# Four graph layers on one core: the nodes' loops taken out of the edge list on chip

## The chip, the cores and the metric
The kernel runs on one core of a Trainium2 chip. The metric is device time in microseconds: before the change the median of three runs is 5938.38 us (5931.77 to 5943.11). The engines are PE (TensorE), DVE (VectorE), ACT (ScalarE), POOL (GpSimd) and SP (SyncE), each with its own instruction stream; they meet at semaphores.

## The reference, cut to what matters
There are 6250 nodes with 256 features. The edge list has 106250 entries, sorted by destination: 100000 random ones (50000 drawn and their reverses) and one loop for each node. The sort is stable and the loops were appended last, so a node's loop is the last entry of that node. Four layers follow one another; each has the form

```
h = max(layernorm(x), 0);  x = x + layer(h, src, dst)
L0 (hyperbolic): agg = segment_sum(logmap(h[src], h[dst]) * edge_weight, dst), then row-wise Moebius steps
L1 (attention):  g = direction * magnitude of h @ W.T + b;  score = g[src] @ a_s + g[dst] @ a_t
                 agg = segment_sum(g[src] * softmax_over_dst(score), dst);  out = ball(g + agg)
L2:              g = h @ W; e = exp(-leaky_relu(g[r] @ a1 + g[c] @ a2, 0.2)); out = elu(sum(e * g[c]) / sum(e))
L3 (mean):       out = h @ w_self.T + b_self + (segment_sum(h[src], dst) / degree) @ w_neigh.T
```
In L0 a loop's term is zero (logmap of a point at itself). In L1, L2 and L3 a loop's term is the node's own row with its own factor.

## The kernel before, in words
Nodes lie in 49 blocks of 128. X (the running x), H (the rows that are gathered or added) and A (the sums) each hold all blocks in SBUF, 256 features wide, H and A with three more columns (AUX to AUX3) for scores, squares and sums of factors.

**Set-up** (DVE from L1001, PE from L494, SP from L331). The list is 831 tiles of 128 edges (ET). A tile that crosses from one block into the next gets one step for each, which makes 831 + 48 = 879 steps, padded to S = 880. DVE builds a matrix `pick` of tiles against steps and PE multiplies the split integers with it (L513) to get the tables src_tab, dst_tab, w_tab and block_tab, one column a step. In the meantime DVE takes the statistics of x (L1064), and ACT normalizes (norm_first, L843) and squares (square_first, L848). SP stores the rows of the first layer to the DRAM table in seven parts (store_part, L361), after it has written the lists of steps out. A is cleared by POOL (L483) when those have landed.

**A pass** is one layer's walk over the steps. In each step POOL gathers the 128 source rows by an indirect DMA out of the table (gathers_layer0, L464, into a ring of 48 slots; gathers, L472, ring of 40), a weighted one-hot matrix of the destinations is made (DVE compares, ACT weighs), PE multiplies it with the gathered rows (sum_step0, L570; sum_step, L577), and DVE adds the product from PSUM to the step's block of A (add_sum, L1133). Where the step starts a new block, the factor same_tab is 0 and the old contents of A are dropped. POOL waits on the semaphore `used`, which PE raises for each ring slot that it has read.

- Pass 1 (L0) works in groups of 16 steps. DVE takes the dot products of gathered rows with own rows two groups ahead (own_dot, L1229), the distances one group ahead (edge_distances, L1250), so the first sum needs two groups of gathers.
- Pass 2 (L1) works in groups of 20 steps. Each group's softmax maxima are found along the rows by scans and linked across rows; a running sum is faded where a block goes on into the next group (fade_first). best_scores (L1534) adds a table not_own that masks a node's own score. In the last 49 steps finished blocks are divided by their totals (totals, L1585) and added to H (combine, L1590), one a step; ACT squares them (square_sum).
- Pass 3 (L2) is alike with its own exponents (leaky_exponents, L1653), and finished blocks go through elu steps on ACT and DVE.
- Pass 4 (L3) needs no weights.

After each pass norm_pipe (L1512) updates X, normalizes, and PE multiplies with the next weights; SP stores the new table. POOL starts the next pass when the seven parts have landed. The order of the work inside a pass is written out by hand, step by step, for each engine.

Of the kernel before, what the change touches and what calls it, by code (L numbers as in the profile page):

```python
# [30 lines left out]
S_REAL = ET + NB - 1  # L31
ITERS = -(-S_REAL // RING)
S = ITERS * RING
assert S - S_REAL <= 1
SH = S // 2
UN = 7
assert ITERS % 2 == 1
# [14 lines left out]
LATE = 17  # L52
# [4 lines left out]
SUM_LAG = HOTS + 2  # L57
# [3 lines left out]
NG0 = S // GR0  # L61
# [6 lines left out]
assert S % GR0 == 0 and SLOTS0 * W <= NB * D and 4 * OWN <= SLOTS  # L68
FAR = 1 << 20
# [7 lines left out]
def gnn_program(nc, x, src, dst, edge_weight, w0, bias0, w1, b1, mag_w, mag_b, attn_w, w2, a2,  # L77
                w_neigh, w_self, b_self, out):
    with ExitStack() as ctx:
# [50 lines left out]
        ident_b = sb("ident_b", [P, P], BF16)  # L130
# [5 lines left out]
        own_dram = nc.dram_tensor("own_dram", [P, S], F32, kind="Internal").ap()  # L136
# [56 lines left out]
        not_own = w_tab[:, :]  # L193
# [19 lines left out]
        fade_1 = e_flat[:, 10 * GR + 9:10 * GR + 10]  # L213
        is_first = e_flat[:, 10 * GR + 10:10 * GR + 10 + NG]
        assert 10 * GR + 10 + NG <= 18 * RING
        pick = a_flat[:, 0:EC * S // 2].bitcast(BF16).rearrange("p (c s) -> p c s", c=EC)
        iota_s = a_flat[:, EC * S:EC * S + S]
        t0_ = EC * S + S
        turned_dst = a_flat[:, t0_:t0_ + EC * P].rearrange("p (c e) -> p c e", c=EC)
        t0_ += EC * P  # L220
        rows_out = a_flat[:, t0_:t0_ + EC * P // 2].bitcast(BF16).rearrange("p (c e) -> p c e", c=EC)
        t0_ += EC * P // 2
        cuts_out = a_flat[:, t0_:t0_ + EC * (P + 2) // 2].bitcast(BF16).rearrange("p (c e) -> p c e", c=EC)
        t0_ += EC * (P + 2) // 2
        own_out = a_flat[:, t0_:t0_ + S]
        t0_ += S
        links_out = a_flat[0:1, t0_:t0_ + 3 * CW // 2].bitcast(BF16).rearrange("p (n s) -> p n s", n=3)
        t0_ += 3 * CW // 2
        assert t0_ <= NB * W and CW % 2 == 0
        o = 0  # L230
        rows_i, parts_of = {}, {}
        for name in ("dst", "src"):
            rows_i[name] = h_flat[:, o:o + EC * P].bitcast(I32).rearrange("p (c e) -> p c e", c=EC)
            o += EC * P
# [84 lines left out]
        def batch_in(eng, q, i, j, ahead=0):  # L319

            eng.wait_ge(sem(f"batch_in{j}"), i * (16 * BATCH) + 16 * BATCH * (q * TURNS + 1 + ahead))
# [170 lines left out]
        def _(pe):  # L492
# [13 lines left out]
            for n, name, made in ((0, "dst", 1), (3, "tile", 1), (1, "src", 2), (2, "w", 3)):  # L506
                pe.wait_ge(sem("parts_made"), made)
                terms = [(t[:, c, :], c) for t in parts_of[name] for c in range(EC)]
                if name == "tile":
                    terms += [(tile_low, c) for c in range(EC)]  # L510
# [1366 lines left out]
```

## Time and profile before
| what | value |
| --- | --- |
| median of 3 runs | 5938.38 us |
| lowest, highest run | 5931.77, 5943.11 us |
| profiled execution, first to last instruction (span) | 5110.8 us |
| own time of the profiled execution beyond the span | not given; the median lies 827.6 us above the span |
| busy PE, DVE, ACT, POOL | 3290.4, 3431.6, 1841.1, 3349.8 us |
| mean granted TensorE clock | 0.810 of full speed |
| gathers (indirect DMAs of POOL) | 3520, 467.01 MB |

A busy share is an average over four passes and the stretches between them, in which different engines work. Which engine ends a stretch has to be read from the waits and from the timeline. DMA issues and semaphore waits are not counted as busy, except POOL's indirect DMAs, whose descriptors POOL makes itself.

### The profile page before, as it was taken

The page shows a single profiled execution, that of the slowest core. Times are in us where ns is not written, and L with a number is a line of the kernel's source. Part 1 is how long each engine was busy: PE and PEld are TensorE (multiplying, and loading weights), DVE is VectorE, ACT ScalarE, POOL GpSimd, SP SyncE. Part 2 cuts the span into 40 slices and gives each one's busy share as a digit, 9 for nine tenths or more (in the row PEclk, how much of TensorE's full clock was granted, in tenths as well). Part 3 has the DMA queues.
Part 4 walks back from the last instruction along what each step waited for, and adds up shares of the span by engine and source line. Part 5 has one row for each costly group of instructions (what it writes and reads, how often), then busy time and mean ns, then how long its engine had stood idle before and what let it go on. Part 6 is the DMA issues. An engine that isn't in the chain of part 4 may idle for free. (4 is left out here: it accounts for less than half of the span.)

```text
span 5110.8 us, 58785 instructions
## 1 busy us (share of the span) xinstructions
PE 3290.4 (64%) x11755; PEld 2256.4 (44%) x11755; DVE 3431.6 (67%) x10603; ACT 1841.1 (36%) x4370; POOL 3349.8 (66%) x3529
## 2 busy tenths in 40 slices
PE   2788888887444655566655666666666666666666
PEld 1556666655332333333334444444444444444444
DVE  7799999999974666666676555555558455555556
ACT  2455555555782333333344333333337100000000
POOL 1777777774007777777752777777772577777776
PEclk7899999998776777777777888888877877778787
DMA  4444444444024333333445554555554444443434
GB/s 137 136 133 132 134 133 133 133 133 120 11 91 124 107 107 107 107 107 107 107 117 153 132 132 132 132 132 134 133 133 141 138 114 114 114 114 107 113 107 142
DMA packets 302511, 617.15 MB, mean 121 GB/s; under 512 B 66649, under 2 KB 175189, under 8 KB 302166
## 3 DMA queue, kind: packets, MB, share of 16 engines
q0 software_dynamic: 168960, 467.01, 34.5%
q1 hardware_dynamic: 107862, 117.55, 7.5%
q10 hardware_dynamic: 25344, 28.85, 2.0%
q8 instruction: 113, 1.85, 0.1%
q14 instruction: 232, 1.90, 0.1%
HBM read 560.58 MB, written 52.57 MB: 120 GB/s over the span
## 5 line engine op out<-in xcount | busy, mean ns | idle before, releaser
L478 POOL DMA_INDIRECT X<-table,src_tab x2640 | 2500.7, 947 | 1360.5 <-issue 752.1
L585 PE MATMUL psum<-X,onehot 128*128 128x259 f32 x5280 | 1847.6, 494 | 905.8 <-ACT onehot L722 333.6
L1142 DVE SCALAR_TENSOR_TENSOR A<-A,same_tab,psum 128x259 f32 x3476 | 1671.8, 481 | 756.9 <-PE psum L585 531.8
L585 PEld LDWEIGHTS psum<-X,onehot 128*128 128x128 f32 x5280 | 1169.2, 241 | 1376.9 <-ACT onehot L722 582.4
L468 POOL DMA_INDIRECT X<-table,src_tab x880 | 836.9, 951 | 280.7 <-issue 251.6
L722 ACT ACTIVATE onehot<-G,zero_col,ecols 128x128 f32<-128x128 bf16 x1760 | 730.0, 481 | 688.9 <-PE psum L585 451.3
L594 PE MATMUL psum<-H,G 128*128 x1760 | 603.1, 429 | 249.6 <-DVE G L1238 196.3
L574 PE MATMUL psum<-X,onehot 128*128 128x259 f32 x1760 | 567.6, 407 | 4.2 <-ACT onehot L722 2.2
L594 PEld LDWEIGHTS psum<-H,G 128*128 128x128 f32 x1760 | 323.7, 205 | 429.0 <-issue 392.1
L722 ACT ACTIVATE onehot<-onehot,zero_col,coef 128x128 f32<-128x128 bf16 x880 | 365.9, 481 | 128.7 <-DVE coef L1281 103.1
L1238 DVE SCALAR_TENSOR_TENSOR G<-psum,X 128x257 f32<-128x257 f32 x880 | 367.1, 418 | 61.8 <-DMA X<-table,src_tab 38.0
L722 ACT ACTIVATE ecols<-ecols,zero_col 128x20 f32<-128x20 f32 (+2 forms) x187 | 52.4, 302 | 987.5 <-DVE ecols L1663 486.9
L574 PEld LDWEIGHTS psum<-X,onehot 128*128 128x128 f32 x1760 | 357.5, 204 | 71.3 <-issue 10.7
L992 ACT COPY onehot<-psum 128x256 f32<-128x256 f32 x49 | 18.2, 372 | 1020.0 <-PE psum L560 1020.0
L1129 DVE TENSOR_TENSOR G<-psum,dst_tab 128x1280 bf16<-128x1280 f32 x176 | 261.3, 1485 | 34.6 <-ACT onehot L722 34.5
L1245 DVE TENSOR_SCALAR onehot<-iota_b,dst_tab 128x128 bf16<-128x128 bf16 x880 | 230.0, 261 | 0.0
L623 PE MATMUL psum<-ident,ecols 128*20 128x128 f32 x44 | 17.0, 387 | 308.5 <-DVE ecols L1539 308.5
L1657 DVE TENSOR_REDUCE ecols<-psum 128x20 f32<-128x60 f32 x44 | 9.7, 221 | 292.0 <-DMA X<-table,src_tab 292.0
L722 ACT ACT_TABLE_LOAD x137 | 175.8, 1283 | 77.5 <-DVE mv L1072 61.3
L1538 DVE TENSOR_TENSOR ecols<-X,w_tab 128x20 f32<-128x20 f32 x44 | 8.2, 186 | 264.3 <-DMA X<-table,src_tab 264.3
L1129 DVE TENSOR_TENSOR onehot<-psum,dst_tab 128x640 f32<-128x640 f32 x176 | 144.1, 819 | 43.6 <-issue 33.4
L616 PE MATMUL psum<-wide_rows,onehot 128*128 x880 | 131.6, 237 | 58.0 <-issue 38.4
(347 smaller groups left out, 2826.0 us busy)
## 6 DMA issues: line engine op xcount, KB each, us to landing
X<-table,src_tab POOLq DMA_INDIRECT x3520, 2.8
plain<-rows_dram SPq DMA_DIRECT2D x110, 256.0 KB
plain<-rows_dram ACTq DMA_DIRECT2D x176, 160.0 KB, 3.4
table<-H SPq DMA_DIRECT2D x21, 906.5 KB, 8.5
x_dram<-X SPq DMA_DIRECT2D x21, 896.0 KB, 4.1
X<-x_dram SPq DMA_DIRECT2D x14, 896.0 KB, 5.1
X<-in_x SPq DMA_DIRECT2D x2, 6144.0 KB
table<-A SPq DMA_DIRECT2D x7, 906.5 KB, 7.2
```

The costliest lines, as they stand in the source:

```text
L468: pool.indirect_dma_start(ring0[:, s % SLOTS0, :], None, table, bass.IndirectOffsetOnAxis(src_tab[:, s:s + 1], 0)).then_inc(sem(f"batch0_{ ...
L478: pool.indirect_dma_start(ring[:, s % SLOTS, :], None, table, bass.IndirectOffsetOnAxis(src_tab[:, s:s + 1], 0)).then_inc(sem(f"batch_in{s ...
L574: pe.matmul(psum[:, s % ACC_BANKS, 0:W], hots0[:, s % HOTS0, :], ring0[:, s % SLOTS0, :], start=True, stop=True).then_inc(sem("used"), 1)
L585: pe.matmul(psum[:, k % ACC_BANKS, 0:W], hots[:, k % HOTS, :], ring[:, k, :], start=True, stop=True).then_inc(sem("used"), 1)
L594: pe.matmul(psum[:, 4 + s % 4, 0:D + 1], oht[:, s // B0 % 2, s % B0, :], blk(H, at, 0, D + 1), start=True, stop=True).then_inc(sem("own_ro ...
L616: ins = pe.matmul(psum[:, 4 + h, c * OWN:c * OWN + P], hot_t[:, first % 2, k, :], u_parts[:, bass.ds(vs[k] * OWN, P)], start=True, stop=True)
L722: return act.activation(out_, in_, f, **kw)
L992: act.copy(late_v, late_turned).then_inc(sem("late_kept"), 1)
L1129: return tt(out_, numbers.rearrange("p (o n) -> p o n", o=1).to_broadcast([P, n, P]), dst_tab[:, bass.ds(first, n)].rearrange("p (s o) -> ...
L1142: stt(total, total, same, psum[:, t % ACC_BANKS, 0:W], ALU.mult, ALU.add).then_inc(sem("sum_added"), 1)
L1238: stt(junk0[:, q, k % 2, at:at + D + 1], psum[:, 4 + s % 4, 0:D + 1], 1.0, ring0[:, s % SLOTS0, 0:D + 1], ALU.mult, ALU.mult, accum_out=en ...
L1245: ts(equal0[:, s % GR0, :], iota_b[:, :], dst_tab[:, s:s + 1], None, ALU.is_equal).then_inc(sem("equal_0"), 1)
```

## The change
The loops are taken out of the list on chip. DVE packs destination-in-block and source of each edge into one word, clears each node's last entry, and moves every word left by the number of loops before it in its block (its destination's number in the block), in seven conditional shifts by 1, 2, 4, ... 64. Every block then loses exactly 128 entries, and what crosses a row's left edge is added to the row before: each of the 830 rows of 128 has edges of one block alone. POOL moves the weights in the same seven rounds with DVE's masks. The rows are turned by PE into the tables. S is 840; pass 1 walks S0 = 832 steps, the others 830.

The own terms come from SBUF: in pass 2 the sums carry their peak in AUX3 and are merged with the node's own row in three groups of blocks (MERGES: 0-14, 14-28, 28-49), in pass 3 ACT writes own rows times own factor into A before the sums, in pass 4 A holds the own rows already; in passes 3 and 4 add_sum always adds (factor 1.0). The set-up is reordered: x is loaded by ACT's queue in seven parts at once, its statistics come part by part after the words are moved, A is cleared first, the four weights are loaded and turned last, and the lists of steps are written out after the table's parts.

```diff
-S_REAL = ET + NB - 1
-S = ITERS * RING
-LATE = 17
+S_REAL = E // P
+LT = -(-(E - N) // P)
+S = 840
+LATE = 16
+MERGES = ((0, 14), (14, 28), (28, NB))
+S0 = 832
+LOW = [P + 1 - (1 << i) for i in range(7)]
 # SP
-            sp.wait_ge(sem("edges_padded"), 6)
-            (dst, src, w: 9 loads; prev_i: 7 loads; then weights, vectors, x in 2 loads)
+            rows_in("dst", dst, dst_rows_i[:, :, 0:P], "edges_in")
+            for c in range(EC): (first number of the next row, 7 loads)
+            rows_in("src", src, src_rows_i, "edges_in")
+            sp.wait_ge(sem("sums_zero"), 1)
+            rows_in("w", edge_weight, w_rows[:, :, P:2 * P], "w_in")
...
 # POOL
+            pool.memset(A[:, :, :], 0.0).then_inc(sem("sums_zero"), 1)
+            def move_weights():
+                pool.wait_ge(sem("w_in"), 16 * 3)
+                pool.wait_ge(sem("words_made"), 1)
+                now = w_rows[:, :, P:2 * P]
+                pool.tensor_tensor(now, now, keep_rows, ALU.mult).then_inc(sem("w_kept"), 1)
+                for i, low in enumerate(LOW):
+                    shift = 1 << i
+                    pool.wait_ge(sem("movers"), i + 1)
...
+                    now, to = w_rows[:, :, low:], w_rows[:, :, low - shift:2 * P - shift]
+                    pool.tensor_copy(moved_w[i], movers[i])
+                    pool.tensor_tensor(moved_w[i], now, moved_w[i], ALU.mult)
+                    pool.tensor_tensor(now, now, moved_w[i], ALU.subtract)
+                    pool.tensor_tensor(to, to, moved_w[i], ALU.add)
...
+            def scale_own(lo, hi):
+                pool.wait_ge(sem("shares"), len(MERGES))
+                for b in range(lo, hi):
+                    pool.tensor_scalar(H[:, b, 0:D], H[:, b, 0:D], col("be")[:, b:b + 1], None, ALU.mult).then_inc(sem("own_scaled_late"), 1)
-            pool.wait_ge(sem("steps_out"), 16 * (2 * EC + 2))
-            pool.memset(A[:, :, :], 0.0).then_inc(sem("sums_zero"), 1)
+            pool.wait_ge(sem("src_kept"), 1)
             pool.wait_ge(sem("table_stored"), 16 * OUTER)
             gathers_layer0()
 # ACT
+            for c in FIRST_ORDER:
+                act.dma_start(X[:, a:z, :], x[a * P:z * P, :]...).then_inc(sem(f"x_part{c}"), 16)
...
+            def merges(s):
+                for m, (lo, hi) in enumerate(MERGES[:-1]):
+                    at = s - (LT + hi)
+                    if at == 4: merge_parts(m)
+                    if 0 <= at - 8 < hi - lo: scale_own(m, lo + at - 8)
+                    if 0 <= at - 14 < hi - lo: square_sum(lo + at - 14)
...
+                    for b in range(NB):
+                        func(A[:, b, :], H[:, b, :], ACT.Identity, scale=col("be")[:, b:b + 1]).then_inc(sem("own_rows"), 1)
 # DVE
-            pick, number_parts, bn_stats of all x, tables from PE's products
+            chain(stt(first, delta_i, float(1 << SRC_BITS), src_rows_i, ALU.mult, ALU.add))
+            chain(stt(first, first, float(REAL << SRC_BITS), keep_rows, ALU.add, ALU.mult))
+            for i, low in enumerate(LOW):
...
+                chain(ts(movers[i], now, SRC_BITS + i, 1, ALU.logical_shift_right, ALU.bitwise_and))
+                chain(tt(taken, now, movers[i], ALU.mult))
+                chain(tt(now, now, taken, ALU.subtract))
+                chain(tt(to, to, taken, ALU.add))
+            first_stats(0)
+            for n in range(1, OUTER):
+                first_stats(n)
+                first_rstd(n - 1)
...
             def add_sum(q, i, t, at, same=None):
+                if q > 0:
+                    same = 1.0
...
             def best_scores(i, h):
-                chain(tt(tg, at[:, :, AUX3], not_own[...], ALU.add))
-                tt(cand, tg, at[:, :, AUX2], ALU.max)
+                dve.tensor_copy(cand, ring[:, h % 2 * GR:h % 2 * GR + GR, AUX2])
...
+            def merge_gaps(m):    (nine operations on lo:hi columns)
+            def merge_shares(m):  (seven operations on lo:hi columns)
+            def merges(s):
+                    if at == 0: merge_gaps(m)
+                    if at == 6: merge_shares(m)
+                    if 0 <= at - 10 < hi - lo: combine(lo + at - 10)
...
-            totals(OUTER - 1)
-            for b in range(S - ET - UN, NB):
-                combine(b)
+            merge_gaps(len(MERGES) - 1)
+            for m, (lo, hi) in enumerate(MERGES[:-1]):
+                for b in range(max(lo, lo + S_REAL - LT - hi - 10), hi):
+                    combine(b)
+            merge_shares(len(MERGES) - 1)
+            for b in range(*MERGES[-1]):
+                combine(b)
```

## Rows read from the trace of the kernel before

**Rows 1.** Groups by line, all of the span: busy us, mean ns | idle us before, releasers.

```profile
L478 POOL DMA_INDIRECT X<-table,src_tab x2640 | 2500.7, 947 | 1360.5 <-issue 752.1 <-DMA table<-H 438.0 <-DMA table<-A 119.2
...
L468 POOL DMA_INDIRECT X<-table,src_tab x880 | 836.9, 951 | 280.7 <-issue 251.6 <-PE psum L574 16.1 <-DMA table<-H 13.0
```

**Rows 2.** Timeline of POOL: start us, us, what [idle before <-releaser].

```profile
126.10 1.11 POOL L468 DMA_INDIRECT X<-table,src_tab  x1 [12.99 <-DMA table<-H]
...
1229.79 0.94 POOL L468 DMA_INDIRECT X<-table,src_tab  x1 [0.30 <-issue]
...
1542.30 0.94 POOL L478 DMA_INDIRECT X<-table,src_tab  x1 [311.57 <-DMA table<-H]
...
2641.25 0.94 POOL L478 DMA_INDIRECT X<-table,src_tab  x1 [0.30 <-issue]
...
2768.63 0.94 POOL L478 DMA_INDIRECT X<-table,src_tab  x1 [126.44 <-DMA table<-H]
...
5091.00 0.95 POOL L478 DMA_INDIRECT X<-table,src_tab  x1 [0.30 <-issue]
```

**Rows 3.** Stretches, passes 1 and 2: busy PE, PEld, DVE, ACT, POOL, clock, DMA.

```profile
171.00:1230.00 1059.00, 875.65 (x3379) 651.79 (x3379) 975.23 (x4380) 616.76 (x1212) 801.91 (x845) 0.93 0.49 132
...
1575.00:2642.00 1067.00, 644.40 (x2035) 390.57 (x2035) 676.66 (x1703) 384.77 (x960) 807.20 (x854) 0.77 0.40 108
```

**Rows 4.** Waits of all engines: us in total, times, longest.

```profile
DVE ecols L1538 <- DMA X<-table,src_tab: 264.3, 44, 19.3
...
DVE G L1238 <- DMA X<-table,src_tab: 38.0, 41, 5.0
```

**Rows 5.** One line, the sums of pass 1: duration ns, first and last start.

```profile
L574 PE MATMUL psum<-X,onehot x1760: 379/382/772, 171.6 to 1259.0; 128*128 128x259 f32 x196
```

**Rows 6.** Timeline of the set-up, DVE, ACT, PE and SP.

```profile
15.12 0.23 DVE L1020 CAST ident_b<-ident 128x128 bf16<-128x128 f32 x1 [10.22 <-DMA H<-in_dst]
...
34.24 0.62 DVE L1039 TENSOR_SCALAR H<-H 128x896 int32<-128x896 int32 x1
...
37.33 1.09 DVE L1058 TENSOR_TENSOR H<-H 128x896 f32<-128x896 f32 x1
...
43.95 16.11 DVE L1064 BATCH_NORM_STATS2 G<-X 128x6 f32<-128x256 f32 x49 [3.74 <-DMA X<-in_x]
...
63.72 3.55 ACT L722 ACTIVATE H<-X,cols 128x256 f32<-128x256 f32 x7 [0.77 <-DVE cols L1075]
...
74.24 1.75 PE L519 MATMUL psum<-ident,dst_tab 128*128 128x128 f32 x7 [14.28 <-DVEq L1093]
...
92.93 6.99 ACT L722 ACTIVATE H<-X,cols 128x256 f32<-128x256 f32 x14 [5.03 <-DVEq L1124]
...
100.54 14.37 SPq L362 DMA_DIRECT2D table<-H  x7
```

**Rows 7.** Timeline around POOL's memset and behind it.

```profile
102.44 10.67 POOL L483 MEMSET A<- 128x12691 f32 x1 [100.04 <-DMA links_dram<-A]
...
102.73 0.42 DVE L1183 SCALAR_TENSOR_TENSOR G<-H 128x256 f32<-128x256 f32 x1
...
103.46 9.69 DVE L1187 COPY cols<-H 128x49 f32<-128x49 f32 x1 [0.30 <-ACT onehot L722]
...
123.19 0.19 DVE L1216 TENSOR_SCALAR cols<-cols 128x49 f32<-128x49 f32 x1
...
125.85 0.21 DVE L1219 COPY H<-cols 128x49 f32<-128x49 f32 x1 [2.47 <-DMA table<-H]
```

**Rows 8.** Timeline, end of pass 2 and start of pass 3.

```profile
2679.00 0.47 DVE L1142 SCALAR_TENSOR_TENSOR A<-A,same_tab,psum 128x259 f32 x1
...
2680.22 2.86 DVE L1591 SCALAR_TENSOR_TENSOR A<-A,cols,H 128x256 f32<-128x256 f32 x7
...
2683.70 0.49 ACT L722 ACTIVATE wide_rows<-A,zero_col 128x256 f32<-128x256 f32 x1
...
2795.51 0.22 DVE L1657 TENSOR_REDUCE ecols<-psum 128x20 f32<-128x60 f32 x1 [15.21 <-DMA X<-table,src_tab]
```

More of the change, by code:

```diff
@@ L268, in blocks_at, with base, batch_turns @@
                 skip_runtime_bounds_check_because="set-up clamps the steps' blocks to NB - 1")[1]
+        def base(q):
+            return S0 + q * S if q >= 0 else 0
+        def batch_turns(j):
+            return sum(i * SLOTS + j * BATCH < S_REAL for i in range(TURNS))
         block = ctx.enter_context(nc.Block())
@@ new lines, in _ @@
+            sp.wait_ge(sem("edges_padded"), 2)
+            rows_in("dst", dst, dst_rows_i[:, :, 0:P], "edges_in")
+            with nc.allow_non_contiguous_dma(reason="one number of each row"):
+                for c in range(EC):
+                    n = min(P, ET - 1 - c * P)
+                    sp.dma_start(dst_rows_i[0:n, c, P:P + 1], dst[(c * P + 1) * P:(c * P + n) * P + 1:P].rearrange("(p c) -> p c", c=1)
+                                 ).then_inc(sem("edges_in"), 16)
+            rows_in("src", src, src_rows_i, "edges_in")
@@ L488, in _ @@
                 gathers(q)
+                if q == 0:
+                    scale_own(*MERGES[-1])
         @block.tensor
@@ L985, in _ @@
             weighted(1)
-            for b in range(S - ET - ELU_LAG, NB + 1):
+            for b in range(S_REAL - LT - ELU_LAG, NB + 1):
                 elu_parts(b)
@@ new lines, in _, with first_stats @@
+            dve.sem_inc(sem("words_moved"), 1)
+            dve.memset(H[:, :, AUX], -0.5)
+            chain(dve.memset(H[:, :, AUX3], 0.0))
+            dve.sem_inc(sem("aux_kept"), 1)
+            def first_stats(n):
+                c = FIRST_ORDER[n]
+                dve.wait_ge(sem(f"x_part{c}"), 32 if c == OUTER - 1 else 16)
+                for b in part(c):
+                    ins = dve.bn_stats(out=stats0[:, b, 0:6], in_=X[:, b, :])
+                chain(ins)
+                now = part_of(stats0, c)
+                m0, m1, v0, v1 = now[:, :, 1], now[:, :, 4], now[:, :, 2], now[:, :, 5]
+                two, odd, off = part_of(col("t0"), c), part_of(col("t1"), c), part_of(col("t2"), c)
+                tt(off, m0, m1, ALU.subtract)
+                tt(odd, v0, v1, ALU.add)
+                chain(tt(two, m0, m1, ALU.add))
+                chain(stt(off, off, 0.25, off, ALU.mult, ALU.mult))
+                stt(mv[:, c * UN:c * UN + UN, 1], odd, 1.0 / D, off, ALU.mult, ALU.add).then_inc(sem("var_ready"), 1)
@@ L1838, in _ @@
             chain(dve.memset(A[:, :, AUX:W], 1.0))
-            for b in range(S - ET - 10, NB):
+            for b in range(S_REAL - LT - 10, NB):
                 weighed(b)
```

595 lines of the change are left out of this document (337 added, 258 removed).

## The prediction
> **What bounds the kernel now.** I read first the costliest groups of the page, and there the gathers: one GpSimd (POOL) indirect DMA per step, 2640 in three passes and 880 in the first, each busy 0.95 us, with nearly all the idle time before them put down to "issue" [rows 1]. Then the timeline of POOL alone, for the first and the last gather of each pass: the first pass runs from 126.10 to 1229.79, so 879 periods of 1.2556 us; the second from 1542.30 to 2641.25, 879 periods of 1.2502 us [rows 2]. The last gather of the kernel starts at 5091.00, 19.8 us before the end of the span. So in all passes POOL issues without a stop, at 0.95 us + 0.30 us of its own issue; a pass costs 880 of these periods. Third, the table of stretches: in the first pass DVE is busy 975 of 1059 us (92%), in the second 677 of 1067 (63%), PE and ACT less [rows 3]. Fourth, the waits: DVE waits 264 us for gathered rows in the second pass and only 38 us in the first [rows 4]. POOL sets the time in every pass; in the first DVE is close behind it: its own pace is about 1.2556 - 38/880 = 1.21 us a step. Between passes POOL is idle 311.6, 126.4 and 119.2 us, and 126 us before the first.
>
> **The steps that go.** The first pass keeps 832 of 880 gathers, the others 830. On the path: 48 x 1.2556 = 60.3 us and 150 x 1.2502 = 187.5 us, together 247.8 us. Nothing else can take their place in passes 2 to 4: in pass 2 the busiest other engine is idle for a third of the time [rows 3], and the page's slices show no more in passes 3 and 4. PE, ACT and DVE lose the same steps; that is worth nothing there.
>
> **Set-up, the part that can give some back.** Before, the table of the first pass is what POOL waits for: the edges are in at 15.1; picking the tiles (DVE 20 to 32) and PE's matmuls run until the input x has landed at 43.9 and its 49 statistics are done at 60.1; ACT normalizes from 63.7 on and is held at the last two parts and a half by the DVE's tables until 92.9; the seven stores of 0.9 MB go out from 100.54 and have landed at 126: 3.6 us each [rows 2, 6].
>
> After, x is asked for at once by ACT's queue, beside the edge lists (13 small DMAs of SP). Before, 15 edge DMAs were in 11 us after the first issue [rows 6]; with x beside them I take 20 us for the words' start (low 16, high 27). Then DVE has seven rounds over 7 chunks of 128, 129, 131, 135, 143, 159, 191 columns: in all 7112 columns, 7.94 times the 896 of the rows shown. A round is one operation with one input (0.63 us for 896) and three with two inputs (1.09 us) [rows 6], 3.9 us; 7.94 x 3.9 + 28 waits of 0.05 = 32 us. POOL does the same rounds on the weights: one copy and three two-input operations. No row has such an operation on POOL. Its nearest row is the memset of 12691 columns in 10.67 us, 0.84 ns each [rows 7]. One stream a column is the low end; two reads and a write one after the other, 2.5 ns, the high end. I take 2.1 for the two-input ones (between two and three streams) and 0.84 for the copy: 7112 x (3 x 2.1 + 0.84) = 51 us; ends: 24 and 60.
>
> **Do the two take turns?** In the trace a DVE copy of 49 columns, which took 0.21 us at 125.85, lasted 9.69 us at 103.46: it started under POOL's memset and ended with it [rows 7]. A two-input DVE operation that started 0.3 us into that memset took its normal 0.42 us [rows 7]. So the one-input operations of the rounds wait for POOL's whole instruction; of the two-input ones the row only says that they don't mind a POOL instruction that merely writes. POOL's rounds read as well. I take it that all take turns, one for one, since both queues chain their steps and each leaves the other a gap: 32 + 51 = 83 us, and the words are moved at about 20 + 83 = 103, the weights at 104. If only the one-input operations wait, it is 20 + 32 + 7 copies of POOL or so = 60, and the weights at 75.
> The Trainium skill, "SBUF — State Buffer", section "SBUF: two separate sides", says that DVE's second pair of ports is GpSimd's only one, an exclusive lock held for a whole instruction, and that a DVE operation with two SBUF inputs contends with a GpSimd operation that reads SBUF. By that rule all the rounds take turns, 83 us and not 40; the trace shows its first half (the 9.69 us), no row here shows the second. "GPSIMD Engine Reference", section "Elementwise — side-by-side cycle accounting", gives 4497 ns for a two-input f32 operation of 2048 columns; by that figure the POOL rounds would be an estimated 53 us.
>
> **First gather.** After the words are moved (103): one part of x's statistics 2.3 (a seventh of 16.11), its small operations 0.9, the second part's of both before the first reciprocal 3.2, reciprocal and start 1 (the root with its table load lies beside it): ACT starts at 111. It has 49 normalizations of 0.51 (7 in 3.55 us) [rows 6] and 21 squares of 0.49 [rows 8], with seven roots 37 us: 148. The last part's store adds 3.6 + 2: the first gather at 154, against 126.1: **+28**.
>
> **First sum.** DVE's own list behind it: 7 parts x 3.7 us of statistics (129), tables 5, the 28 row squares, which end with ACT's order at about 141, the block row 4, so the tables stand at 145. From there before, at 74.2, to the cuts kept at 92.9 it was 18.7 us [rows 6]; it gets two more matmuls and four row operations (+5), then the weights' turn and table 6, the four weight copies 3 (moved from the front), and the chain of small operations that took 10.0 us from 113.2 to 123.4 [rows 7]. That is 145 + 43 = 188, 34 us after the first gather. Before, DVE stood ready at the first gather and the first sum came 45 us later (171.6) [rows 5], held by 32 gathers. Now the 32 gathers are there, and DVE, PE and ACT need by their own pace about 36 us: the first sum at 224. POOL's ring of 48 is full at 154 + 60 = 214, and it goes on when four sums are done, at 228: **+14**. From there on 784 periods of 1.2556: the last gather at about 1212, against 1229.8. DVE's 1.21 us a step lets it keep up. So of 60.3 us the first pass gives 18 and the set-up eats 42 (bounds from the unknowns: 0 with no turns at all, 60 with 2.5 ns and edges at 27).
>
> **Between second and third pass.** Before, the last sum ends at 2679.5, 7 sums are combined until 2683.1, ACT's last square is done at 2684.2 [rows 8], 43 us after the last gather. After, the last merge group is 21 blocks and all of it comes behind the last sum. The last sum itself stays near 38 us after the last gather: the last group has 10 steps, not 20, but ACT has per step a weighing, a scaling and a square, 1.46 us instead of 0.97. Then nine small DVE operations (1.7), two exponentials (0.7), seven more (1.4), and 21 blocks at POOL's pace: 256 columns, 0.3 us at the memset's rate, 0.65 at 2.1 ns, and DVE's 0.48 us combine (two inputs) either beside it or in turn with it: 10 to 24 us; I take 15, plus the last square 1. Sum 38 + 3.8 + 15 + 1 = 58 against 43: **+14** (5 to 24).
>
> **Start of the third pass.** 49 own rows on ACT, 49 x 0.51 = 25 us, from about 2774 on in the old count: done at 2799. The exponents wait for 20 gathers anyway until 2795.5 [rows 8]. 3 us late, and POOL's ring of 40 has 50 us: **0**. If that cover were gone it would be 25.
>
> **At no cost.** The extra operations of a group in pass 2 (a copy, two one-column operations) lie in DVE's 37% idle time, with 6 us of waiting for gathers in each of 44 groups [rows 3, 4]. End of passes 3 and 4: the same 48 or 49 blocks follow the same last gathers; ACT bounds the tail of pass 3 before and after (0, at most -5 or +5). Pass 4: one more mean behind its last sum, +0.5.
>
> **Sum.** -247.8 + 42 + 14 + 0.5 = -191 us on the profiled execution, whose span is 5110.8; the page gives no other time of it. The median of the runs is 827.6 us more than this span. What lies there isn't in the trace; I take it as unchanged: 5938.4 - 191 = **5747 us**, span 4920. If it goes with the number of steps, it loses up to 198/3520 of 828 = 47 us.
>
> **Rivals.** (1) No turns, or few: the two-input operations of DVE and POOL run side by side. For: the 0.42 us row. Against: POOL's rounds read, the memset doesn't. The words are at 60, all behind is 43 us earlier, total 5704. (2) DVE is the bound of the whole first pass: it starts 34 us behind POOL and 92% busy; if its pace is 1.2556 and not 1.21, the last sum comes at 224 + 1045 = 1269 instead of 1241: 5775. For: 92%. Against: the 38 us it waits. (3) The steps are free for POOL but the time around the span shrinks with the program: 5700. Nothing in the profile speaks for or against. (4) Slower: POOL's moving of the weights. It is one chain in set-up, and every sum waits for its last step. Break-even is where it takes 191 us more than my 51: 242 us for 28448 columns, 8.5 ns a column, ten times the memset's rate. For: none of these forms is in the trace, POOL is a slow engine for them if they convert and overlap in place. Against: 0.84 ns in the only row. It gives over 5940, by 12 ns 6040. (5) It doesn't do what it says, POOL's period grows as gathers of empty slots (6250 of them, all to row 0) hit one row: needs 1.25 to 1.31 us. Against: the time from a gather's issue to its data is not on POOL.
>
> **Chances.** Forecast 0.60 (own range 5725 to 5770); rival 1 0.20; rival 2 0.10; rival 3 0.06; rivals 4 and 5 together 0.04. Range: down to rival 1 and a little of 3, up past rival 2 and POOL at 2.5 ns with late edges: 5685 to 5795. A measurement of this kernel tells 0.2% (12 us) from no change. Faster by more: 0.95; within: 0.02; slower: 0.03.
>
> **What would show it.** Right: 832 and 3 x 830 gathers at 1.25 us without waits but for one of some 14 us at the 49th; DVE's two-input operations in the rounds at 2 to 3 us instead of 1.09 to 1.6; first gather near 154, first sum near 224; the gap between passes 2 and 3 near 140 us. Wrong: DVE's rounds at normal length (rival 1); waits of POOL for PE all through pass 1 (rival 2); a POOL operation of over 8 us in the rounds (rival 4); the span 191 us shorter but the time by another amount (rival 3).

## The result, and the profile after

| runs | before, us | after, us | ratio |
|---|---|---|---|
| first timing | 5935.08 (5924.34 to 5943.11) | 5719.18 (5710.40 to 5728.73) | 0.9635 [0.9619, 0.9652] |
| later (experiments 1 and 2) | 5108.73 (5106.85 to 5112.72) | 4942.97 (4942.24 to 4945.48) | 0.9675 [0.9662, 0.9689] |

After is 216 us faster in the first timing, where 191 were predicted. The second line is from the experiments, and it changes how the first is read. Some executions are held up again and again for some 3 us at a time, here called stops; others, of the same kernel, never are. The trace of before that stood ahead of the prediction (span 5110.8 us) is of an execution without stops, while its runs took 5935 us; from the experiments it follows that the 827.6 us that the prediction put "around the span" are such stops, though no trace of before holds them. The first trace of after has them: its span is 5726.9 of its 5728.73 us. This is its timeline of all engines in one stop of the second pass (start, length, engine, line, operation, tiles, in brackets the idle time before and what ended it):

```profile
2501.58 0.30 PEld L639 LDWEIGHTS psum<-X,onehot 128*128 128x128 f32 x2 [1.44 <-issue]
2502.09 0.95 POOL L519 DMA_INDIRECT X<-table,src_tab  x1 [0.30 <-issue]
2505.05 1.26 ACT L780 ACTIVATE onehot<-G,zero_col,ecols 128x128 f32<-128x128 bf16 x3 [3.39 <-remote]
2505.22 1.11 DVE L1280 SCALAR_TENSOR_TENSOR A<-A,same_tab,psum 128x259 f32 x2 [2.36 <-remote]
2505.33 0.94 POOL L519 DMA_INDIRECT X<-table,src_tab  x1 [2.29 <-remote]
2505.82 0.50 PEld L639 LDWEIGHTS psum<-X,onehot 128*128 128x128 f32 x2 [3.95 <-ACT onehot L780]
```

ACT, DVE, POOL and PE all start again within 0.8 us, after 2.3 to 4 us. The releaser "remote" says only that no record of the releaser is there: the traces with stops hold 24600 to 25900 records of semaphore updates, those without 77600 to 81600. Of the intervals between POOL's gathers within the passes, 300 are over 2 us; the median stays 1.254. In 298 of the 300 the next gather is one ahead of which POOL waits on the semaphore `used` (in pass 1 every fourth from the 49th on, later every fifth); the other two are among the first ten gathers. So POOL is held at its waits and not at any place, and the other engines are not always still then: during 138 of the 300 all of them start nothing for 1.5 us or more, during 117 one of them starts something at least every 1 us.

The second trace of after (span 4943.4 us) has no stops and is the one to lay beside the rows of before. Its page and its costliest groups on POOL:

```profile
span 4943.4 us, 56247 instructions
PE 3104.0 (63%) x11120; PEld 2145.1 (43%) x11120; DVE 3249.0 (66%) x10287; ACT 1807.0 (37%) x4285; POOL 3270.2 (66%) x3382
...
L519 POOL DMA_INDIRECT X<-table,src_tab x2490 | 2372.3, 953 | 1273.5 <-issue 711.3 <-DMA table<-H 396.0 <-DMA table<-A 119.6
L509 POOL DMA_INDIRECT X<-table,src_tab x832 | 794.5, 955 | 307.9 <-issue 235.8 <-DMA table<-H 50.8 <-PE psum L626 21.3
```

These answer to [rows 1]: 2490 + 832 gathers instead of 2640 + 880, each still 0.95 us. POOL's timeline in that trace, the first and last gather of each pass and the 49th of the first, answers to [rows 2]:

```profile
155.59 1.21 POOL L509 DMA_INDIRECT X<-table,src_tab  x1 [50.79 <-DMA table<-H]
222.18 0.94 POOL L509 DMA_INDIRECT X<-table,src_tab  x1 [3.63 <-PE psum L626]
1206.22 0.95 POOL L509 DMA_INDIRECT X<-table,src_tab  x1 [0.30 <-issue]
1518.52 0.94 POOL L519 DMA_INDIRECT X<-table,src_tab  x1 [311.36 <-DMA table<-H]
2554.91 0.95 POOL L519 DMA_INDIRECT X<-table,src_tab  x1 [0.30 <-issue]
2713.15 1.01 POOL L519 DMA_INDIRECT X<-table,src_tab  x1 [84.66 <-DMA table<-H]
3760.11 0.95 POOL L519 DMA_INDIRECT X<-table,src_tab  x1 [0.31 <-issue]
3880.62 0.95 POOL L519 DMA_INDIRECT X<-table,src_tab  x1 [119.56 <-DMA table<-A]
4924.65 0.95 POOL L519 DMA_INDIRECT X<-table,src_tab  x1 [0.31 <-issue]
```

From these starts and those of before comes the ledger (us, from first to last gather for a pass, from last to first for a gap):

| stretch | before | after | change | predicted |
|---|---|---|---|---|
| to the first gather | 126.1 | 155.6 | +29.5 | +28 |
| pass 1 | 1103.7 | 1050.6 | -53.1 | -60.3 + 14 = -46 |
| gap 1 to 2 | 312.5 | 312.3 | 0 | 0 |
| pass 2 | 1099.0 | 1036.4 | -62.6 | -62.5 |
| gap 2 to 3 | 127.4 | 158.2 | +30.9 | +14 |
| pass 3 | 1102.2 | 1047.0 | -55.2 | -62.5 |
| gap 3 to 4 | 120.6 | 120.5 | 0 | 0 |
| pass 4 | 1099.6 | 1044.0 | -55.6 | -62.5 |
| behind the last gather | 19.8 | 18.8 | -1.0 | +0.5 |
| sum (span) | 5110.8 | 4943.4 | -167 | -191 |

The gap between passes 2 and 3 is off by 17 us, passes 3 and 4 by 7 us each, and pass 1 by 7 the other way. The other 50 us of the 216 are stops: they cost before 5935.1 - 5108.7 = 826 us and after 5719.2 - 4943.0 = 776.

### The profile page after: what moved, and what is told of

Same layout as the page of the kernel before. It is cut to its first block and busy times, and to the rows that moved or that the text cites. A ratio compares the mean times of both kernels' runs of the same rounds, so it can differ in the third digit from the quotient of the medians.

```text
span 5726.9 us, 56247 instructions
## 1 busy us (share of the span) xinstructions
PE 3325.1 (58%) x11120; PEld 2190.7 (38%) x11120; DVE 3240.2 (57%) x10287; ACT 1822.4 (32%) x4285; POOL 3263.8 (57%) x3382
## 3 DMA queue, kind: packets, MB, share of 16 engines
q0 software_dynamic: 159456, 440.74, 29.5%
## 5 line engine op out<-in xcount | busy, mean ns | idle before, releaser
L519 POOL DMA_INDIRECT X<-table,src_tab x2490 | 2367.9, 951 | 1799.0 <-issue 695.8
L639 PE MATMUL psum<-X,onehot 128*128 128x259 f32 x4980 | 1917.1, 525 | 1270.9 <-DVE A L1280 621.5
L639 PEld LDWEIGHTS psum<-X,onehot 128*128 128x128 f32 x4980 | 1130.2, 253 | 1848.1 <-issue 1055.4
L1280 DVE SCALAR_TENSOR_TENSOR A<-A,psum 128x259 f32 x1660 | 701.6, 423 | 1325.8 <-remote 723.0
L1280 DVE SCALAR_TENSOR_TENSOR A<-A,same_tab,psum 128x259 f32 x1620 | 776.8, 480 | 579.4 <-remote 259.0
L509 POOL DMA_INDIRECT X<-table,src_tab x832 | 792.6, 953 | 535.2 <-issue 232.0
L780 ACT ACTIVATE onehot<-G,zero_col,ecols 128x128 f32<-128x128 bf16 x1660 | 699.3, 482 | 994.6 <-remote 324.9
L626 PE MATMUL psum<-X,onehot 128*128 128x259 f32 x1664 | 557.8, 421 | 4.4 <-DVE A L1280 3.1
L780 ACT ACTIVATE onehot<-onehot,zero_col,coef 128x128 f32<-128x128 bf16 x832 | 350.4, 482 | 275.3 <-DVE coef L1411 93.2
L626 PEld LDWEIGHTS psum<-X,onehot 128*128 128x128 f32 x1664 | 353.8, 214 | 74.2 <-issue 9.5
L1368 DVE SCALAR_TENSOR_TENSOR G<-psum,X 128x257 f32<-128x257 f32 x832 | 346.9, 417 | 17.4 <-remote 8.4
L814 ACT CAST G<-G 128x1024 f32<-128x1024 bf16 x104 | 107.8, 1037 | 180.0 <-PE psum L648 85.5
L670 PEld LDWEIGHTS psum<-wide_rows,onehot 128*128 128x128 bf16 x840 | 83.2, 104 | 155.1 <-issue 132.4
```

The source lines that it names most:

```text
L509: pool.indirect_dma_start(ring0[:, s % SLOTS0, :], None, table, bass.IndirectOffsetOnAxis(src_tab[:, s:s + 1], 0)).then_inc(sem(f"batch0_{ ...
L519: pool.indirect_dma_start(ring[:, s % SLOTS, :], None, table, bass.IndirectOffsetOnAxis(src_tab[:, s:s + 1], 0)).then_inc(sem(f"batch_in{s ...
L626: pe.matmul(psum[:, s % ACC_BANKS, 0:W], hots0[:, s % HOTS0, :], ring0[:, s % SLOTS0, :], start=True, stop=True).then_inc(sem("used"), 1)
L639: pe.matmul(psum[:, k % ACC_BANKS, 0:W], hots[:, k % HOTS, :], ring[:, k, :], start=True, stop=True).then_inc(sem("used"), 1)
L670: ins = pe.matmul(psum[:, 4 + h, c * OWN:c * OWN + P], hot_t[:, first % 2, k, :], u_parts[:, bass.ds(vs[k] * OWN, P)], start=True, stop=True)
L780: return act.activation(out_, in_, f, **kw)
```

## The experiments

After's time without stops is 4942.97 us; "gap" is the one between passes 2 and 3, 158.2 us in after.

**1. Before again, unchanged.** 

> The kernel before, unchanged, once more, for a second trace. In the trace shown of before the span is 5110.8 us though the kernel's runs take about 5935, and none of its intervals between gathers in a pass is over 1.6 us; in the trace of after the span is 5726.9 of 5728.7 us, and all engines stop together about 300 times for some 3 us (711.9 us beyond 1.25 us a gather, and more in the gaps). Theory A: every timed execution holds such stops, and the first trace of before was of an execution without them: the span is now 5925 to 5945 us, a pass of 880 gathers lasts 1240 to 1360 us instead of 1100 to 1104, the stops hold 700 to 830 us, and an average step costs 1.43 to 1.50 us where the prediction took 1.25. Theory B: the 827.6 us lie around the span in before's executions as the prediction took it: the span is again about 5111 us, with no interval over 1.6 us, and a step costs 1.25 us.

Span 5118.2 us, no interval over 1.6 us, a step 1.253 to 1.260 us: B's numbers. But before's nine timed runs beside it had a median of 5108.73, so nothing lies around the span and B's reason is wrong; A is wrong in that not every execution has stops. At three later times, each on another chip, before's median was 5107.7, 5869.5 and 5922.0. Each chip was met once, so whether the chip makes the stops, or something else that changed between the times, is not shown.

**2. After again, unchanged.** 

> The kernel after, unchanged, timed beside the next two kernels, and for a second trace. 5710 to 5729 us (0.9635 of before). If the stops of all engines come at places fixed by the program, passes 1 to 4 last 1276, 1203, 1222 and 1196 us again, each within 3 us; if they come by the clock of the chip, single passes differ by more and the sum stays.

4942.97 us and not the expected 5710 to 5729, since no execution here had stops; the ledger above is its trace. Whether stops come at fixed places it can't tell; later traces say no: of the 71 and 68 pauses over 2 us in pass 3 of experiments 8 and 12, 29 follow the same gather, as many as chance would give among 166 places. With the stops of the first trace the passes took 1275.6, 1203.4, 1221.5 and 1196.0 us: 225, 167, 175 and 152 more than here, while the gaps grew by 10 to 15 us each and the end by 29.

**3. POOL's rounds after VectorE's.**

```
     pool.tensor_tensor(now, now, keep_rows, ALU.mult).then_inc(sem("w_kept"), 1)
+    pool.wait_ge(sem("words_moved"), 1)
     for i, low in enumerate(LOW):
```

> After with POOL's seven rounds begun only when VectorE's are done. Nothing is left out. Theory turns: words moved at 60 to 63 us, POOL's rounds from there alone beside the statistics and square rows, done at 115 to 125 us, first gather at 122 to 132 us, and the tables, which wait for the weights, stand no later than in after (147 us): time 15 to 32 us below after's. Rival: the turns only move, POOL's 51 us of rounds and VectorE's statistics take turns instead and the first gather comes at 145 to 155: time within 8 us of after's. Rival, no turns at all: POOL's rounds end at 115, VectorE's at 95: time 0 to 10 us above after's.

4934.17 us, 0.9650 [0.9637, 0.9663]: 9 us below after, where 15 to 32 were expected. First the timeline of after without stops, in the third round (VectorE, then POOL in the same stretch), then that of this kernel in the same round, its first small statistics (7 columns) and POOL beside them:

```profile
43.98 1.11 DVE L1134 TENSOR_SCALAR A<-A 128x917 int32<-128x917 int32 x1
45.12 2.58 DVE L1135 TENSOR_TENSOR onehot<-A 128x917 int32<-128x917 int32 x1
47.85 2.59 DVE L1138 TENSOR_TENSOR A<-A,onehot 128x917 int32<-128x917 int32 x1
50.47 2.75 DVE L1139 CUSTOM_DVE_ANT_0 A<-A,onehot 128x1834 uint16<-128x1834 uint16 x1
...
43.12 1.62 POOL L495 CAST A<-A 128x903 f32<-128x903 int32 x1
44.82 1.91 POOL L497 TENSOR_TENSOR A<-A 128x903 f32<-128x903 f32 x1
...
52.39 1.65 POOL L495 CAST A<-A 128x917 f32<-128x917 int32 x1
```

```profile
39.98 1.11 DVE L1135 TENSOR_SCALAR A<-A 128x917 int32<-128x917 int32 x1
41.12 1.12 DVE L1136 TENSOR_TENSOR onehot<-A 128x917 int32<-128x917 int32 x1
42.38 1.11 DVE L1139 TENSOR_TENSOR A<-A,onehot 128x917 int32<-128x917 int32 x1
43.53 1.12 DVE L1140 CUSTOM_DVE_ANT_0 A<-A,onehot 128x1834 uint16<-128x1834 uint16 x1
...
77.01 1.79 DVE L1164 SCALAR_TENSOR_TENSOR cols<-cols 128x7 f32<-128x7 f32 x1
78.83 0.17 DVE L1165 SCALAR_TENSOR_TENSOR mv<-cols 128x7 f32<-128x7 f32 x1
78.92 0.19 DVE L1171 RECIPROCAL cols<-cols 128x7 f32<-128x7 f32 x1
79.14 1.70 DVE L1172 SCALAR_TENSOR_TENSOR cols<-cols 128x7 f32<-128x7 f32 x1
...
74.88 1.91 POOL L498 TENSOR_TENSOR A<-A 128x903 f32<-128x903 f32 x1
76.87 1.91 POOL L500 TENSOR_TENSOR A<-A 128x903 f32<-128x903 f32 x1
78.86 1.97 POOL L502 TENSOR_TENSOR A<-A 128x903 f32<-128x903 f32 x1
80.95 0.95 POOL L496 CAST A<-A 128x917 f32<-128x917 int32 x1
...
146.21 1.21 POOL L510 DMA_INDIRECT X<-table,src_tab  x1 [24.56 <-DMA table<-H]
```

A two-input operation of DVE takes 1.12 us alone and 2.58 beside POOL. The one-input one (L1134) takes 1.11 either way, though POOL's instruction beside it is mostly a conversion; the reciprocal at 78.92, 0.19 us under a two-input operation of POOL (78.86), shows it cleanly. POOL waits too: its conversion took 1.65 us beside DVE's two-input operation at 50.47 and takes 0.95 alone. But the expected 122 to 132 us for the first gather was wrong: it came at 146.2, the rival's value. The turns only move. DVE's rounds end 29 us sooner, and then operations of 7 columns, 0.17 us by themselves, start under a POOL operation of 1.9 us and end with it (78.80, 80.84), two or three times for each part of the statistics.

**4. No rounds on POOL.**

```
-    for i, low in enumerate(LOW):
-        ...
+    pool.sem_inc(sem("w_kept"), 1)      # 14 times, one after the other
```

> After without POOL's seven rounds that move the weights (the weights then stand in wrong places, the rest of the work is the same). Theory turns, with what the run with the words first showed (VectorE's rounds alone took 37.4 us, 29.1 to 66.5; in after they take 66.6, to 95.3): words moved at 66 to 67 us, small operations of the statistics 0.2 us each and none at 2 us, first gather at 124 to 129 us where after has 155.3, VectorE ready for its first sum earlier by as much, and 26 to 31 us less than after's time (0.9675 of before: 4943 beside 5108.7; this run 0.9615 to 0.9625). Rival (VectorE's rounds are long by themselves): excluded by the run with the words first. Rival, the ring: the gathers start 29 us earlier but VectorE is ready less than 15 us earlier, POOL waits with its ring full for over 15 us where it waited 3.3, and the time is less than 15 us below after's.

4913.53 us, 0.9618 [0.9603, 0.9632]: 29.4 us below after, in the 26 to 31 of the theory. The kernel leaves out the rounds, so its weights stand in wrong places. The first gather is at 123.86 (31.7 sooner) and the wait of the 49th is 3.9 us, in after 3.6: what the first gather gains, the pass keeps. So the moving of the weights costs all of the +28, and more; without it set-up would be no later than before's 126.1.

**5. 196 gathers more.**

```
+    if s % 17 == 8:
+        pool.wait_ge(sem("again_in"), 16 * again[0])
+        pool.indirect_dma_start(spare_rows[:, :], None, table, ...).then_inc(sem("again_in"), 16)
```

> After with 49 gathers more in each pass (every seventeenth is issued twice, the second into rows that nothing reads), 196 in all; no other engine does more. Theory POOL bounds each pass (the prediction's: a step is worth what its gather takes on POOL): 196 x 1.252 = 245 us more than after, so 5188 us beside 5108.7 of before (ratio 1.0155). Rival, the other engines bound passes 1 and 3 for part of the time (their pace is 1.264 and 1.263, above 1.250 in pass 2): added gathers then hide in part, 225 us or less, ratio 1.0115 or less. Rival, the transfers queue up: over 255 us, ratio over 1.0175.

5181.67 us, 1.0146 [1.0130, 1.0161]: 238.7 more than after, between the 245 of the theory and the 225 of its rival and nearer to the first. The four passes grew by 57.2, 61.3, 60.7 and 60.5 us; 49 x 1.2502 is 61.3. A gather that POOL issues is worth its whole period in passes 2 to 4, and in the first all but 4 us: its wait for the first sums falls from 3.6 us to 0.4.

**6. No scaling of own rows in pass 2.**

```
-    func(H[:, b, 0:D], H[:, b, 0:D], ACT.Identity, scale=col("be")[:, b:b + 1]).then_inc(sem("own_scaled"), 1)
+    act.sem_inc(sem("own_scaled"), 1)
...
-    pool.tensor_scalar(H[:, b, 0:D], H[:, b, 0:D], col("be")[:, b:b + 1], None, ALU.mult)...   # 21 blocks
+    pool.sem_inc(sem("own_scaled_late"), hi - lo)
```

> After without the scaling of the nodes' own rows before they are merged at the end of pass 2 (28 on ACT while the pass runs out, 21 on POOL after it; the merged rows are then wrong). In after the last sum of the pass starts 48.7 us after its last gather where before had 37.8 (ACT has 1.37 us of work a step there: hot rows, own rows, squares), the group's chain of shares ends at 53.2, and POOL's 21 blocks at 73.6. Theory of the gap 2 to 3 (both parts are late because of the scaling): last sum again at 37 to 40 us, last square at about 37.8 + 5.3 + 21 x 0.6 = 56, so the gap from last gather to first gather falls from 158.2 us to 138 to 142, and the time by 16 to 20 us. Rival, only POOL's part counts: last sum stays at 48 to 49, the gap falls to 149 to 151 us. Rival, the stores and the turning of blocks behind it set the end: gap within 3 us of 158.

4913.57 us, 0.9619 [0.9605, 0.9634]: 29.4 us below after, where 16 to 20 were expected. The kernel leaves out the scaling. The gap is 143.8 us, 14.5 less (2 short of the expected range); the last sum starts 41.9 us after the last gather instead of 48.7. Of the other 15 us, 13 are in passes 3 and 4, 1040.3 and 1037.3 us instead of 1047.0 and 1044.0, which no theory had foreseen. The end of pass 2 in after without stops, from the last sum to the last square, and then the last sum of this kernel:

```profile
2603.61 0.48 DVE L1280 SCALAR_TENSOR_TENSOR A<-A,same_tab,psum 128x259 f32 x1 [0.49 <-PEq L732]
2604.60 0.18 DVE L1723 TENSOR_SCALAR cols<-A 128x21 f32<-128x21 f32 x1
2609.29 0.18 DVE L1744 TENSOR_SCALAR cols<-cols 128x21 f32<-128x21 f32 x1
2609.57 18.92 POOL L527 TENSOR_SCALAR H<-H,cols 128x256 f32<-128x256 f32 x21 [53.71 <-DVE cols L1744]
2627.63 0.70 DVE L1751 SCALAR_TENSOR_TENSOR A<-A,cols,H 128x256 f32<-128x256 f32 x1 [0.20 <-POOL H L527]
2628.53 0.48 DVE L1751 SCALAR_TENSOR_TENSOR A<-A,cols,H 128x256 f32<-128x256 f32 x1 [0.20 <-POOL H L527]
2629.05 0.51 ACT L780 ACTIVATE wide_rows<-A,zero_col 128x256 f32<-128x256 f32 x1
```

```profile
2591.64 0.48 DVE L1279 SCALAR_TENSOR_TENSOR A<-A,same_tab,psum 128x259 f32 x1
```

**7. The last group's rows on POOL and ACT** (15 and 6 blocks).

```
+    for b in range(43, NB):              # ACT, ahead of its squares
+        scale_own(len(MERGES) - 1, b)
...
-    scale_own(*MERGES[-1])               # POOL
+    scale_own(MERGES[-1][0], 43)
```

> After with the last group's 21 own rows split: POOL scales the first 15, ACT the last 6 (0.39 us each) ahead of its squares. Nothing is left out. Theory: POOL 15 x 0.9 = 13.5 us and ACT 2.4 + 21 x 0.6 = 15 us stand where POOL's 18.9 + 1.5 stood: the gap 2 to 3 falls from 158.2 to 152 to 154 us, and the time by 4 to 6 us (less than 3 rounds could tell). Rival, ACT's squares follow at their old pace of 0.9 us because VectorE's combining beside POOL (0.70 us each where it takes 0.48 alone) sets it: gap 157 to 159.

4940.45 us, 0.9668 [0.9655, 0.9682], beside 0.9675: the times don't tell the two apart. In the trace the gap is 155.4 us, 2.9 less and short of what was expected: POOL ends 5.4 us sooner, but DVE has six blocks left to combine then, which the sum had left out.

**8. POOL free of the last group.** VectorE scales 14 blocks, ACT 7.

```
+    def scale_late(b):                   # VectorE, one block ahead of combine(b)
+        ts(H[:, b, 0:D], H[:, b, 0:D], col("be")[:, b:b + 1], None, ALU.mult).then_inc(sem("own_scaled_dve"), 1)
...
-    if q == 0:
-        scale_own(*MERGES[-1])           # POOL
```

> After with POOL freed of the last group's 21 own rows: VectorE scales 14 of them, one ahead of each combining, ACT the last 7. Nothing is left out. In every trace with POOL's scaling the gathers of passes 3 and 4 took 952.6 ns each beside 945.5 in passes 1 and 2, and without it (the run that leaves the scaling out) 945.9 in pass 3. Theory A: POOL's scaling itself makes each later gather 7.2 ns longer: passes 3 and 4 last 1040 and 1037 us again instead of 1047 and 1044, 12 to 13 us less; beside that the 21 blocks take about 16 us instead of 20.5, so the gap 2 to 3 is 153 to 155 us. Time 15 to 19 us below after's, ratio to before 0.9640 to 0.9648. Theory B: the longer gathers have another cause that leaving out the scaling changed too (ACT's work, the place of the code): passes 3 and 4 keep 952.6 ns, and the time is only 3 to 6 us below after's.

This experiment and all behind it met executions with stops, so times are read as ratios: 0.9629 [0.9612, 0.9647], not to be told from after's 0.9635. What tells is the length of a gather. The rows are the gathers of one pass each (ns min/median/max, first and last start). In after without stops, passes 2, 3 and 4:

```profile
L519 POOL DMA_INDIRECT X<-table,src_tab x830: 942/946/1041, 1518.5 to 2554.9; - x166
L519 POOL DMA_INDIRECT X<-table,src_tab x830: 949/953/1322, 2713.2 to 3760.1; - x166
L519 POOL DMA_INDIRECT X<-table,src_tab x830: 947/953/1174, 3880.6 to 4924.7; - x166
```

With no scaling at all (experiment 6), pass 3; and in this kernel, pass 3:

```profile
L519 POOL DMA_INDIRECT X<-table,src_tab x830: 942/946/1330, 2693.5 to 3733.8; - x166
```

```profile
L520 POOL DMA_INDIRECT X<-table,src_tab x830: 943/949/1102, 3078.8 to 4274.7; - x166
```

Here pass 2 had a median of 949 too. The median of a whole trace is 946 or 949 (before's two traces have one each), so what counts is a step between passes 2 and 3, and here there is none, as theory A has it.

**9. One block on POOL.** As 8, with POOL's range of one block and VectorE's of 13. 

> As the run before, but POOL scales one block (the first of the 21), VectorE 13 and ACT 7. Nothing is left out. Theory A1, a state that POOL's first such instruction leaves behind: gathers of passes 3 and 4 take 952.6 ns each, as with 21 blocks, and the time is 11 to 13 us above the run before's. Theory A2, it grows with the number of instructions: 945.5 + 7.2/21 = 946 ns, time within 3 us of the run before's. Theory B (another cause): no difference between the two either way.

0.9623 [0.9603, 0.9642]. Medians 949 and 949 in passes 2 and 3: one such instruction leaves nothing behind (A1 is out). But A2 doesn't hold either: with 15 blocks (experiment 7) pass 3 has 953, as with 21, where in proportion it would have 951.

**10. Another form on POOL.**

```
-    pool.tensor_scalar(H[:, b, 0:D], H[:, b, 0:D], col("be")[:, b:b + 1], None, ALU.mult)
+    pool.tensor_tensor(H[:, b, 0:D], H[:, b, 0:D], col("be")[:, b:b + 1].to_broadcast([P, D]), ALU.mult)
```

> After with POOL's 21 blocks as a product of two tensors (the column spread over the row) instead of a tensor and a scalar. Nothing is left out. POOL's seven rounds of set-up are of that two-tensor form, and the gathers after them took 946.3 ns. Theory, the form matters: gathers of passes 3 and 4 take 945 to 947 ns, time 10 to 13 us below after's if a block still takes 0.9 us. Theory, any work of POOL between gathers that are counted does it (in set-up no gather had run before): 952.6 ns again, time within 4 us of after's.

0.9631 [0.9610, 0.9653]. The rows are this kernel's passes 2 and 3:

```profile
L519 POOL DMA_INDIRECT X<-table,src_tab x830: 940/946/957, 1736.0 to 2925.7; - x166
L519 POOL DMA_INDIRECT X<-table,src_tab x830: 940/946/1097, 3085.6 to 4282.6; - x166
```

No step: the form decides. A block took 0.77 us on POOL in this form and 0.91 in the other. All other traces agree: those in which POOL ran 15 or 21 operations of the first form have the step from 946 to 953, experiments 11 and 12, in which it ran none, have not.

**11 and 12. Together.** Experiments 3 and 8 in one kernel, and the seven conversions on ACT:

```
+    for i in range(len(LOW)):            # ACT, before its first root
+        act.wait_ge(sem("movers"), i + 1)
+        act.copy(moved_w[i], movers[i]).then_inc(sem("w_cast"), 1)
```

> The version that the runs point to: POOL free of the last group's rows (as two runs before), its rounds of set-up after VectorE's (as the run with the words first), and the seven conversions of a mask in them done by ACT, which idles there. Nothing is left out. POOL's rounds then are 3 instructions each, 47 us instead of 55, from 66.6 to about 114; the stalled small operations of VectorE's statistics end 8 us sooner, the first gather comes at 138 to 142 us (146.2 with the words first, 155.3 in after). Sum: 17 for the freed POOL, 9 for the words first, 3 to 7 for the conversions: 4910 to 4916 us, ratio to before 0.961 to 0.9625. Rival: the ring is full longer because VectorE's readiness moves less than the first gather: conversions bring nothing, 4917 to 4921 us.

> The version of the run before once more (POOL free of the last group's rows, its rounds of set-up after VectorE's, the conversions on ACT; nothing left out), since that run met the stops of all engines that the first runs of before and after held (before 5869.5 us there, 5108 without stops) and after was not timed beside it. If this run is without stops: passes 3 and 4 last 1037 to 1040 us, first gather at 143 to 146 us, gap 2 to 3 of 152 to 155 us, 4910 to 4918 us and 0.9612 to 0.9628 of before, where after had 0.9675 [0.9662, 0.9689]. Rival, that its gain in the run before (0.9602) came of the stops: over 0.965. If this run has stops again: 0.959 to 0.962, and it stands beside after's 0.9635 [0.9619, 0.9652] of its first timing, which had them too.

0.9602 [0.9585, 0.9620] (5630.84 beside before's 5869.5) and 0.9599 [0.9585, 0.9614] (5684.78 beside 5922.0), both with stops; after's in its first timing, with before at 5935, is 0.9635 [0.9619, 0.9652]. The intervals of the second and of after's don't meet, so this version seems to beat after too, by some 21 us (0.0036 x 5935). That is not a measured difference: after wasn't timed beside it, and what the stops cost differs from time to time (before 5869.5, 5922.0 and 5935). First gathers at 144.4 and 142.3 us, beside 146.2 with the words first alone: the conversions brought 2 to 4 us, less than the first expectation had.

## Why the prediction was right, and where it was not

**The steps that go, 247.8 us.** Right: pass 2 lost 62.6 us for 62.5, and experiment 5, which puts 196 gathers back on POOL alone, costs 238.7. POOL bounds every pass.

**Turns in set-up.** Right, and shown by experiments 3 and 4. The Trainium skill, "SBUF — State Buffer", section "SBUF: two separate sides", has the exclusive lock for two-input operations: this case's trace agrees, 1.12 us alone and 2.58 beside POOL. The prediction's own inference from [rows 7], that the rounds' one-input operations wait as well, was wrong: 1.11 us with and without POOL. The sums: the rounds began at 28.8 for 20 and DVE's were done at 95.2 for 103, so they took 66.4 us for 83 (alone DVE's take 37.4 for 32 and POOL's 55 for 51, but they overlap in part: DVE's seven one-input operations, 8.5 us, wait for nobody). The first gather came at 155.6 for 154, but that nearness is luck: the words were 8 us early and the way behind them 9 us longer (60 us for 51). The prediction had ACT end that way at 148, with 5.6 us for the last store. These rows of after without stops, ACT's last square, DVE's last row square and the seven stores, show another end:

```profile
140.60 0.49 ACT L780 ACTIVATE plain<-H,zero_col 128x256 f32<-128x256 f32 x1
144.65 0.42 DVE L1201 SCALAR_TENSOR_TENSOR G<-H 128x256 f32<-128x256 f32 x1
L379 SPq DMA_DIRECT2D table<-H x7: 360/360/908, 112.8 to 145.6; - x7
DMA to landing us min/median/max: 4.5/5.7/9.1
```

ACT was done at 141, but four of the stores wait for DVE's row squares, which stand behind its tables, and the last store, issued at 145.6, needed 9.1 us. At most 3 of the 9 us are DVE's small statistics that ran into POOL's last round (one of 7 columns took 2.6 us).

**First sum and the ring, +14.** Mis-sized: the first sum started at 218.7, not 224, and the 49th gather waited 3.3 us more than its 0.3. Pass 1 ended 7 us better than its term and not 11, since its gathers were 4 ns longer in the mean than before's (955 for 951, 3 us in all).

**Gap 2 to 3, +14.** The mechanism is right, the size is not: +30.9. The step that failed is "the last sum itself stays near 38 us after the last gather": it had ACT's weighing, scaling and square per step at 1.46 us and let it cost nothing, but ACT paces PE and DVE there at 1.37 us a step, POOL's period is 1.25 and the lag grows, so it came at 48.7 (+11). The last group's blocks took 18.9 us on POOL where 15 were taken: this is POOL's own pace, since the first block took 0.93 us with DVE idle and the others 0.91 with DVE's combine (0.70 us for 0.48) beside them. The chain of shares took 5.5 where 3.8 were taken. In us: +11, +4 and +2. Experiment 6 gives back 6.8 of the first, and 7.7 of what lies behind the last sum; ACT's squares remain there.

**Passes 3 and 4, 7 us each.** The prediction kept 1.2502 us a step. The gathers got 7 ns longer (946 to 953) once POOL had run its 21 scalings; nothing in the profile of before could show it. Experiments 6, 8 and 10 tie it to that work and its form.

**What lies around the span, unchanged.** This is the step that was wrong in kind. It was no time around the program but stops inside it, and it fell by 50 us; the 47 us that the prediction named as possible (rival 3) came, on top of 166 where it had 191. That the total of 216 is as near to 191 as it is, is luck: the errors of +24 and -50 stand against each other. Why stops fell from 826 to 776 (0.939) is not shown; the number of gathers fell to 0.944, that of instructions to 0.957, the time without stops to 0.9675. Most of them lie in the passes (719 of 783 us in after's first trace), few in the gaps.

**Rivals.** No turns (1): excluded, 2.58 against 1.12 us. DVE bounds the first pass (2): excluded, experiment 5, and its last sum began at 1236, not 1269. Rounds of POOL that cost 191 us more (4): its two-input operations took 2.74 us for 1337 columns alone, 2.05 ns each, and in turn with DVE's at most 3.56 us for 1113, 3.2 ns each, where 8.5 would have been needed. POOL's period grows (5): it did, by 7 ns and not by the empty slots.

## What to carry to other kernels

A step is worth the period of the engine that bounds the loop, and only that; it can be priced from one row and checked by putting the same instructions back on that engine alone. Two-input work on VectorE beside GpSimd's gains little (92 us of rounds took 76): each operation, however small, waits for the rest of the other's instruction, so keep what VectorE does meanwhile to one input where that is possible. A sum can come out right over a path that is wrong (here the first gather): check what ends the wait, not only when. When the profile's span and the timed runs differ by a lot, don't take the difference as a constant: ask for a second trace first.

## What the runs showed of the hardware that was not expected

- At some times, each on another chip, the same program is held up some 300 times in 5.7 ms, 776 us in all; at others it never is (4943 us). POOL's pauses over 2 us are nearly all at its semaphore waits (298 of 300), and the traces with them hold a third of the semaphore records. The cause is open, and whether the recording of the execution has a part in it isn't tested.
- After 15 or 21 tensor-by-scalar operations on POOL (128x256 f32) its 1660 later gathers took 953 ns in the median instead of 946, to the end of the program; after one such operation, or 21 of two tensors, it did not. Why is open.
- A two-input VectorE operation of 7 columns, 0.17 us alone, took up to 2.6 us beside POOL's two-input operations; a one-input one took its 0.19 us there.
